# Fourier layers on one core: half of the inverse transform along the height as 64x64 quarters of TensorE

## What is computed

```
x = coords @ fc0_w + fc0_b                       # 3 -> 32 channels, then (B, C, H, W)
for sw, cw, cb in four layers:
    x_ft = rfft2(x, norm='ortho')                # over H and W
    out  = einsum('bixy,ioxy->boxy', x_ft[:, :, :20, :20], sw)
    out_ft = zeros; out_ft[:, :, :20, :20] = out
    x1 = irfft2(out_ft, s=(H, W), norm='ortho')
    x2 = einsum('bchw,oc->bohw', x, cw) + cb
    x  = gelu(x1 + x2)
x = gelu(x @ fc1_w + fc1_b); x @ fc2_w + fc2_b
```

## Time and profile before

| | |
|---|---|
| median of 3 runs | 6450.11 us |
| the profiled execution, whole | 6453.83 us |
| its span, first to last instruction | 6452.0 us |
| PE busy | 5726.8 us (89%) |
| PEld busy | 4383.7 us (68%) |
| DVE, ACT, POOL busy | 2856.1, 2673.7, 1098.8 us |
| mean granted TensorE clock | 0.942 |

### The profile page before, as it was taken

The page is one execution under the profiler, slowest core; times in us unless marked ns, Lnnn a source line. Parts: engine busy times, 40 slices in busy tenths (PEclk is TensorE's granted clock), DMA queues, the critical chain, the costliest instruction groups (busy, mean ns, idle before and its releaser), DMA issues. The chain is left out here.

```text
span 6452.0 us, 236091 instructions
## 1 busy us (share of the span) xinstructions
PE 5726.8 (89%) x100782; PEld 4383.7 (68%) x100782; DVE 2856.1 (44%) x4430; ACT 2673.7 (41%) x5007; POOL 1098.8 (17%) x1049
## 2 busy tenths in 40 slices
PE   5999999999899899899999999999999588888888
PEld 4887788678868886887688768877886333333343
DVE  2444344344434443443344334434443565657573
ACT  2334433433353335333433343344334455555563
POOL 3220222032202221221222122203220000000000
PEclk9999999999999999999999999999999788888887
DMA  2101100111011110111010110111000100000000
GB/s 32 13 13 14 19 13 13 14 18 13 13 17 16 16 20 9 16 20 13 13 19 13 14 19 13 13 14 16 13 13 4 20 1 8 1 7 1 4 1 4
DMA packets 442836, 82.80 MB, mean 13 GB/s; under 512 B 437592, under 2 KB 437864, under 8 KB 441704
## 3 DMA queue, kind: packets, MB, share of 16 engines
q1 hardware_dynamic: 441832, 67.58, 8.4%
HBM read 63.33 MB, written 4.23 MB: 10 GB/s over the span
## 5 line engine op out<-in xcount | busy, mean ns | idle before, releaser
L217 POOL COPY x_T<-x_X 128x512 f32<-128x512 f32 x1024 | 1069.6, 1104 | 3744.7 <-ACTq L718 3573.5
L713 ACT ACTIVATE x_X<-ga 128x512 f32<-128x512 f32 x1280 | 752.1, 598 | 888.1 <-PE ga L433 679.4
L591 DVE COPY x_X<-ev 128x512 f32<-128x512 f32 x640 | 442.8, 692 | 1284.7 <-PE ev L451 1214.5
L433 PEld LDWEIGHTS ga<-pw_rhs,x_X 64*64 64x64 f32 x32768 | 605.7, 135 | 293.0 <-issue 291.1
L681 ACT ACTIVATE V<-ga 104x512 f32<-104x512 f32 x416 | 248.4, 597 | 1050.7 <-PE ga L401 1050.7
L401 PE MATMUL ev<-inv_h,D 104*104 104x128 f32 x4864 | 621.1, 277 | 36.9 <-DVE D L591 35.9
L591 DVE COPY V<-ev 104x512 f32<-104x512 f32 x608 | 420.6, 692 | 477.1 <-PE ev L401 477.1
L433 PE MATMUL ga<-pw_rhs,x_X 64*64 64x64 f32 x32768 | 601.0, 218 | 19.4 <-issue 16.9
L401 PEld LDWEIGHTS ev<-inv_h,D 104*104 104x104 f32 x4864 | 562.9, 172 | 73.6 <-DVE D L591 27.0
L463 PEld LDWEIGHTS ev<-dft_consts,x_T 128*64 128x64 f32 x16384 | 575.6, 137 | 47.7 <-issue 47.7
L463 PE MATMUL ev<-dft_consts,x_T 128*64 128x80 f32 x16384 | 594.9, 233 | 10.1 <-POOL x_T L217 9.4
(11 more groups left out here) (195 smaller groups left out, 7638.9 us busy)
## 6 DMA issues: line engine op xcount, KB each, us to landing
mix_w<-in_sw SPq DMA_DIRECT2D x128, 400.0 KB, 8.2
coords<-in_coords SPq DMA_DIRECT2D x64, 96.0 KB, 2.1
maps<-Y SPq DMA_DIRECT2D x128, 16.0 KB
raw<-maps SPq DMA_DIRECT2D x8, 256.0 KB, 3.5
out<-out_t SPq DMA_DIRECT2D x8, 256.0 KB, 3.2
w<-in_w SPq DMA_DIRECT2D x3, 512.0 KB, 6.8
fc_rhs<-in_fc_w SPq DMA_DIRECT2D x32, 0.4 KB
dft_consts<-in_dft SPq DMA_DIRECT2D x1, 336.0 KB
```

The lines of the kernel that those rows point to most:

```text
L217: pool.tensor_copy(x_T[:, :, H * bc + h0:H * bc + h0 + 16].rearrange("p c (s n) -> p c s n", n=2), blocks.rearrange("p (s a n c) -> p a c ...
L433: last = pe.matmul(ps[HALF * bp:HALF * bp + HALF, HALF * s:HALF * s + HALF], x_X[r:r + HALF, g, col:col + HALF], pw_rhs[r:r + HALF, :], st ...
L591: dve.tensor_copy(dst, src).then_inc(ev_taken, 1)
L713: x_new = act.activation(blocks.rearrange("p (s a n) -> p s a n", s=8, a=2)[:, :, bc, :], ga[n % N_GA][:, :].rearrange("p (s n) -> p s n", ...
```

## The change

The old `inverse_h` is kept as `inverse_h_rows` and still serves the first group of each mid layer and the whole last layer. A new `inverse_h` serves the inverse for groups 1, 2 and 3 of the mid layers: 3 groups x 3 layers x 8 chunks = 72 calls. Its first half (channels 0 to 15, banks 0 to 3) is as before, with a no-op after each wait. Its second half works in pairs of banks, one ev and one ga, one for each row half bp. Each pair takes 8 channels, and for each channel there are four matmuls: contraction over 40 rows, 64 or 40 output partitions, 64 columns. The number of banks, of copies and their order on DVE and ACT stay. A copy of the second half takes 64 heights x 8 channels instead of 128 heights x 4 channels.

```
+                def inverse_h(d_at):
+                    pe.wait_ge(ev_taken, ev0 + d_at[0] + 1)
+                    pe.wait_ge(ga_taken, ga0 + d_at[1] + 1)
+                    for i in range(INV_T // 2):
+                        ps = ga_tile() if i % 2 else ev_tile()
+                        passed()
+                        for s in range(4):
+                            last = pe.matmul(ps[0:HALF + KR, P * s:P * s + P], D[0:HALF + KR, 4 * i + s, 0:HALF + KR],
+                                             inv_h[0:HALF + KR, :], start=True, stop=True)
+                        last.then_inc(ga_ready if i % 2 else ev_ready, 1)
+                    for i in range(INV_T // 4, INV_T // 2):
+                        pair = [ev_tile()]
+                        passed()
+                        pair.append(ga_tile())
+                        passed()
+                        for s in range(8):
+                            for bp, ps in enumerate(pair):
+                                r = HALF * bp
+                                for bc, m in enumerate((HALF, KR)):
+                                    last = pe.matmul(ps[HALF * bc:HALF * bc + m, HALF * s:HALF * s + HALF],
+                                                     D[r:r + KR, 8 * i + s, HALF * bc:HALF * bc + m],
+                                                     inv_h[r:r + KR, r:r + HALF], start=True, stop=True)
+                                if s == 7:
+                                    last.then_inc(ga_ready if bp else ev_ready, 1)
 DVE:
+                    inverse_h_rows(2, INV_T // 2)
+                    for i in range(INV_T // 2, INV_T, 2):
+                        n0, c0 = HALF * (i % 2), 8 * (i // 2)
+                        take(V[0:HALF + KR, n0:n0 + HALF, c0:c0 + 8],
+                             ev_tile()[0:HALF + KR, :].rearrange("p (c n) -> p n c", n=HALF))
 ACT:
+                    m = inverse_h_rows(INV_T // 2)
+                    for i in range(INV_T // 2 + 1, INV_T, 2):
+                        act.activation(V[0:HALF + KR, HALF:P, 4 * i - 4:4 * i + 4],
+                                       ga[m % N_GA][0:HALF + KR, :].rearrange("p (c n) -> p n c", n=HALF), ACT.Copy)
```

More of the change, by code:

```diff
@@ L392, in turn_d, with inverse_h_rows @@
                     return n["ev"], n["ga"]
-                def inverse_h(d_at, shared=True):
+                def inverse_h_rows(d_at, shared=True):
                     pe.wait_ge(ev_taken, ev0 + d_at[0] + 1)
@@ L403, in inverse_h @@
                         last.then_inc(ga_ready if shared and i % 2 else ev_ready, 1)
+                    return n["ev"], n["ga"]
+                def inverse_h(d_at):
[22 more added lines that the diff above has]
+                                    last.then_inc(ga_ready if bp else ev_ready, 1)
                     return n["ev"], n["ga"]
@@ L522, in last_group @@
                         fc1(1)
-                        v_next = inverse_h(d_at, shared=False)
+                        v_next = inverse_h_rows(d_at, shared=False)
                     else:
@@ L539, in run @@
                     passed()
-                    v_at = inverse_h(turn_d(0))
+                    v_at = inverse_h_rows(turn_d(0))
                 if kind == "first":
@@ L616, in turn_d, with inverse_h_rows, inverse_h @@
                             take(D[:, :, k0:k0 + 16], bank.rearrange("p (k c) -> p c k", c=CH))
-                def inverse_h(step=2):
-                    for i in range(0, INV_T, step):
+                def inverse_h_rows(step=2, end=INV_T):
+                    for i in range(0, end, step):
                         take(V[0:HALF + KR, :, 4 * i:4 * i + 4],
                              ev_tile()[0:HALF + KR, :].rearrange("p (c n) -> p n c", n=P))
+                def inverse_h():
+                    inverse_h_rows(2, INV_T // 2)
[3 more added lines that the diff above has]
+                             ev_tile()[0:HALF + KR, :].rearrange("p (c n) -> p n c", n=HALF))
                 def turn_x(g):
@@ L649, in run @@
                     turn_d(2)
-                    inverse_h()
+                    inverse_h_rows()
                 else:
@@ L659, in run @@
                         forward_w()
-                    if more:
-                        inverse_h(1 if kind == "last" else 2)
+                    if more and kind == "last":
+                        inverse_h_rows(1)
+                    elif more:
+                        inverse_h()
                     if kind != "last":
@@ L675, in run, with inverse_h_rows @@
                 n = 0
-                def inverse_h():
+                def inverse_h_rows(end=INV_T):
                     m = n
-                    for i in range(1, INV_T, 2):
+                    for i in range(1, end, 2):
                         act.wait_ge(ga_ready, ga0 + m + 1)
@@ L682, in inverse_h @@
                                        ga[m % N_GA][0:HALF + KR, :].rearrange("p (c n) -> p n c", n=P), ACT.Copy)\
+                            .then_inc(ga_taken, 1)
+                        m += 1
+                    return m
+                def inverse_h():
+                    m = inverse_h_rows(INV_T // 2)
+                    for i in range(INV_T // 2 + 1, INV_T, 2):
+                        act.wait_ge(ga_ready, ga0 + m + 1)
+                        act.activation(V[0:HALF + KR, HALF:P, 4 * i - 4:4 * i + 4],
+                                       ga[m % N_GA][0:HALF + KR, :].rearrange("p (c n) -> p n c", n=HALF), ACT.Copy)\
                             .then_inc(ga_taken, 1)
@@ L704, in run @@
                         n += 1
-                    n = inverse_h()
+                    n = inverse_h_rows()
                 for g in range(NG):
```

## The result

The changed kernel takes 6424.16 us, the median of 10 runs (6409.1 to 6433.33), against 6450.48 us for the kernel before in the same rounds (10 runs, 6440.57 to 6456.38). The ratio is 0.9957 with a 95% interval of 0.9949 to 0.9965. So it is faster by 26 us, a quarter of the gain that was forecast (102 us, to 6348), and the range (6310 to 6400) does not hold it. The profiled execution took 6416.93 us.

What follows compares the result with a forecast made beforehand. PE was taken to bound the stage. From 6453.83 us, -103 (quarters), +11 (supply in the groups) and -10 (mix) gave 6352 profiled, 6348 after taking off 3.7; range 6310 to 6400.

Steps and rivals of the forecast that it cites:

- PE sets the pace of this stage: inverse_h: PE busy for 7.20 of 7.20 us, DVE and ACT waiting, so what PE saves moves everything behind it forward.
- The quarters, 1.43 us a call, 103 us: Second half of inverse_h: 3.59 us becomes 1.88 plus 0.28 for tiling switches; 72 calls save 103 us (91 to 123).
- The estimate of 25 ns a record: Quarter matmuls: an estimate from the skill's 60 cycles each at 2.4 GHz, which would leave next to no gain.
- The copies are covered: DVE and ACT copies (0.87 and 0.60 us) keep up with a pair of banks every 0.94 us; forward_h, 2.92 us, covers delays.
- The supply in the groups, +11 us: inverse_h to turn_x: instruction supply holds without slack; 0.15 us more stops a call, bounds -0.1 and 1.33.
- The prediction's first rival: Instruction supply binds: each call stops 0.5 to 1.33 us in forward_h or inverse_w; 6373 to 6434 us, chance 0.15.
- The range: Whole kernel: 6310 to 6400 us, holding the forecast's cases and the nearer part of the supply rival's.
- the two supply terms: Instruction stops in the groups (+11 us) and in the loop's mix (-10 us); between them -25 to +30 us.
- The mix in the loop, -10 us: Mix: the packet edge near its end moves earlier, 0.4 us less in each of 24 mixes, bounds -0.3 and 0.9.
- The clock, unchanged: Low stretch, 1.2 GHz from near mix's end through turn_d, left unchanged; a shift could be 12 us either way.
- Sum: Whole kernel: 6453.83 - 103 + 11 - 10 = 6352 us profiled, 6348 after taking off 3.7.

Runs made afterwards that it cites:

- in turn: Changed kernel with the halves alternating: quarters for channels 0 to 7, rows 8 to 15, quarters 16 to 23, rows 24 to 31; 6403.61 us, ratio 0.9920.
- all channels on quarters: Changed kernel with all 32 channels of the middle groups' inverse on quarters, four pairs of banks and no rows; 6606.79 us, ratio 1.0251.
- 58, 58, 52: Changed kernel with 58, 58 and 52 no-ops on PE in groups 1, 2 and 3 of mid layers, ahead of turn_d; 7040.77 us, ratio 1.0913.
- 168: Changed kernel with 168 no-ops on PE in group 3 of each mid layer, ahead of its forward_w; 7040.92 us, ratio 1.0917.
- narrow surplus: Changed kernel with 14 two-column surplus matmuls at the head of the quarters in each of 72 calls; 6545.06 us, ratio 1.0144; written out 6514.01 us, 1.0100.
- the length alone: Kernel before with 25 no-ops behind each of the eight banks of inverse_h in the 72 calls; 8377.32 us, ratio 1.2985.
- quarters first: Changed kernel with the halves swapped: quarters for channels 0 to 15, then rows for 16 to 31; 6455.07 us, ratio 1.0002.
- The two written-out kernels with equal places: Changed kernel, and the one with quarters and rows alternating, each with the mid-layer loop written out; 6403.94 us (0.9925) and 6378.39 us (0.9883).
- the four pairs of a looped and a written-out kernel: Mid-layer loop written out in four kernels: before 6420.56 us, changed 6403.94, with 14 two-column surplus matmuls 6514.01, quarters and rows alternating 6378.39.
- dense surplus matmuls: Changed kernel with the first of the quarters' eight steps done three times per pair of banks, 16 more matmuls a call; 6438.87 us, ratio 0.9979.

## Why the prediction was wrong

Its steps one by one:

- **PE sets the pace of this stage.** Right. No row of the changed kernel shows DVE or ACT late for the quarters, and forward_h starts at once.
- **The quarters, 1.43 us a call, 103 us.** Nearly right: 1.27 us a call, 91.6 us, which is the lower bound given (91). The stage takes 5.84 us at least (3.67 + 2.17), where 3.58 + 1.88 + 0.28 = 5.74 was forecast, and 5.89 on average, the last 0.05 being its own stops. The estimate of 25 ns a record that the Trainium skill leads to (TensorEngine Tiling, Instruction Overhead) does not agree with the trace, which has 17 ns with the switches included, at the full clock.
- **The copies are covered.** Right; inverse_w waits for V 27.9 us in all (32 times), as before the change, and no row of the waits names a copy for the quarters.
- **The supply in the groups, +11 us.** This step failed in size. forward_h and the inverse_w stages have +32 us (24.4 + 13.3 - 5.7), 0.44 us a call instead of 0.15. The working added up a whole stretch from inverse_h to turn_x (3.8 packets against 16.1 us of work) and called it no slack but enough. An average over so long a stretch hides what happens between two edges. The runs bear that out: the same instructions in another order (in turn) take the 24 us out of forward_h and 34 out of inverse_w, and with all channels on quarters every call has stops. Quarters and forward_h together have 427 instructions in 5.1 us, 3.1 us for 256, which is faster than the packets come; that sum was there to be made from the earlier trace rows. It does not price every call, though. Behind the inverse for group 1 nothing is lost; for groups 2 and 3 the two stages behind are up by 0.71 and 1.13 us. The prediction's first rival had the mechanism and its lower price, 0.5 us a call, and got 0.15.
- **The range.** The term's own bounds, -0.1 to 1.33 us a call, hold the 0.44. But 1.33 us a call would be 96 us, and the range of the forecast allows the two supply terms together only -25 to +30. They came to +59.
- **The mix in the loop, -10 us.** This step failed in its sign and is the largest error: +27.2 us. It was reasoned that the edge near the mix's end moves earlier and its stop vanishes. The edges did move, but now two packets instead of one are asked for around the jump. In the second mix of the first chunk they start 10.1 and 11.1 us into it and take 1.6 and 2.1 us each; before it was one, at 10.9, that took 1.0. All 16 mixes with a jump have the two in the changed kernel, one of 16 had them before. The three kernels that have the old position at the mix (58, 58, 52; 168; narrow surplus) have 427 to 433 us; those that have the new one in the loop (the changed kernel; the length alone, which has no quarters; quarters first; in turn) have 448 to 458. So the place decides here. That a late packet at the jump is what the place costs is argued from these rows, and it is not all: the fourth mix of a chunk, which has no jump, grew by 0.9 us. The bounds given, between 0.3 us longer and 0.9 us shorter a mix, left out the loss that happened in the loop's mixes, 1.3 us.
- **The clock, unchanged.** Not so, and it is tied to the step before. The mean of the span is the same (0.941 for 0.942), but mixes spend 52 us more at 1.2 GHz (126 for 74). The kernel with the halves in turn tells the parts roughly, by one profile each. It has the changed kernel's places, and its mixes spend 74 us at 1.2 GHz, as before the change, and take 447.9 us. So some 18 of the 27 us are there without more of the low clock, and the other 9 go with it. The two written-out kernels with equal places agree: 438.0 us with 141 us at the low level, 425.5 with 76.
- **Sum.** 11 us are missing in the gain of the stage, 21 in the groups' stops, 37 in the mix, 70 of the 76 us between forecast and result. The rest is the scatter between a profiled execution and the median (that of the changed kernel is 7 us below its median, that of before was 3.7 above), less 4.5 us that other stages lost.

What the Trainium skill says of packet edges, that crossing one is mostly hidden (Runtime: NRT & Kernel Launch, Instruction fetch mechanics), was taken in the prediction as not agreeing with the stops, and yet the two supply terms were set so that their sum was about zero, as that rule would have it. The same section says that a taken branch breaks the sequential prefetch. That agrees with the written-out kernels: in the four pairs of a looped and a written-out kernel here, the mixes with a jump lose 1.3 to 2.2 us (2.0 in the kernel before). It would have been the reason to price the mix upwards.

What stays open: why the calls for groups 2 and 3 pay and the one for group 1 does not. In the call for group 1 PE goes from the edge inside the quarters to the next one, in forward_h, in 2.3 us without a stop, after 6.6 us for the 256 instructions before; in the one for group 2 it takes 6.1 us and then 3.3, 0.3 of it a stop. A budget over a single packet does not tell these apart. And no run separates the jump in a mix from the place of the edges beside it.

## What to carry to other kernels

When a change swaps few large instructions for many small ones, compare its pace with the pace of the instruction packets over a few hundred instructions, not over a whole layer. Work that runs faster than its packets can stop the engine, and whether it does depends on where the packet edges fall: here the first of three calls kept the whole gain of 1.6 us, the second 0.6 us of it and the third next to nothing. So split a change's gain by call before naming its cause. Moving the edges with dense filler cost more than it saved; placing sparse work between the dense pieces made all three nearly alike with no instruction added, a ratio of 0.9920 instead of 0.9957. What is added far ahead of a loop's jump can still lengthen the stage around it, so look at the jump in the profile after every change of the code's length.

## What the runs showed that I had not expected

- A no-op with a semaphore on PE costs 0.12 to 0.15 us when many follow each other (14400 lengthened their stage by 1739 us, 4032 the kernel by 617 us). As filler they are dearer than the dense surplus matmuls.
- Fourteen f32 matmuls with two columns, all in one quarter of the array, cost 1.79 us a call, 0.128 us each, whereas sixteen over all four quarters with 64 columns cost 0.63 us (2.846 against 2.221), 0.039 each.
- Short stops cost more than their length. After stops of 1 to 2 us within the quarters, or after the narrow matmuls, the next stage ran at 1.2 GHz in many calls (66 of 72 with all channels on quarters, 42 with the narrow matmuls, 15 with the quarters first): forward_h some 4.4 instead of 2.92 us, the rows 6.7 instead of 3.67.
- Writing out a loop of three iterations gained 27 us in the kernel before, as much as the change under study did.
